# A graph network on one core: 38 of 98 edge groups of the second pass summed by dense one-hot products instead of gathered rows

## The reference, cut to what matters

```python
# 6250 nodes of 96 features, 100000 edges sorted by dst, 32 edge attributes
def L0(x, src, dst, edge_attr):
    edge_input = concat([x[src], edge_attr])
    messages = gelu(edge_input @ mW1 + mb1) @ mW2 + mb2
    gates = sigmoid(gelu(edge_input @ gW1 + gb1) @ gW2 + gb2)
    aggregated = segment_sum(messages * gates, dst)
    update = gelu(concat([x, aggregated]) @ uW1 + ub1) @ uW2 + ub2
    return layernorm(x + update) * ln_g + ln_b
def L1(x, src, dst, edge_weight):            # GCN layer, with self loops
    dinv = rsqrt(segment_sum(edge_weight, dst) + 1)
    return dinv * segment_sum(edge_weight * (x * dinv)[src], dst) @ W + self_loop_term + b
x = layernorm(x + L0(x, ...)); return layernorm(x + L1(x, ...))
```

## Time and profile before

| what | value |
|---|---|
| median of 3 runs | 2140.92 us (2139.51 to 2141.7) |
| the profiled execution's own time | 2138.67 us |
| span of the profile, first to last instruction | 2136.8 us |
| TensorE busy in the span | 1028.7 us (48%) |
| VectorE busy | 952.5 us (45%) |
| ScalarE busy | 388.2 us (18%) |
| GpSimd busy | 1599.9 us (75%) |
| mean granted TensorE clock | 0.678 of full speed |

### The profile page before, as it was taken

One profiled execution on the slowest core, in us unless ns is written; L12 is line 12 of the kernel. 1 busy time (PEld: TensorE's weight loads), 2 busy tenths in 40 slices (PEclk: granted clock), 3 DMA queues, 4 the chain that ended last, 5 costly groups with the idle time before them and its releaser, 6 DMA issues.

```text
span 2136.8 us, 22553 instructions
## 1 busy us (share of the span) xinstructions
PE 1028.7 (48%) x6513; PEld 960.2 (45%) x6514; DVE 952.5 (45%) x3023; ACT 388.2 (18%) x926; POOL 1599.9 (75%) x1577
## 2 busy tenths in 40 slices
PE   1378776767676676767732223322223332222223
PEld 1368776666666666656622222222222222222222
DVE  4248755565656565656641332323333232323323
ACT  1135433333333333333310000000000000000000
POOL 7777777777777777777627777777777777777775
PEclk9789988888888888888865555555555555555555
DMA  5222222222222222222201111211111111111111
GB/s 133 70 59 59 55 52 51 53 51 50 55 49 54 49 52 52 52 51 53 49 18 40 40 41 40 41 41 40 41 41 41 41 40 40 42 40 41 40 40 34
DMA packets 72963, 103.13 MB, mean 48 GB/s; under 512 B 42525, under 2 KB 44093, under 8 KB 72735
## 3 DMA queue, kind: packets, MB, share of 16 engines
q0 software_dynamic: 50048, 76.97, 17.1%
q10 hardware_dynamic: 18288, 17.26, 2.8%
q1 hardware_dynamic: 4496, 7.34, 1.2%
HBM read 96.65 MB, written 4.82 MB: 47 GB/s over the span
## 4 chain that ended last, share of the span: by engine, by line
POOL 74%; issue 22%; PE 1%; DVE 1%; DMA 0%; DVEq 0%; ACT 0%; POOLq 0%; ACTq 0%
POOL rows L299 74%; PE ps_win L350 0%; PE ps_hid L404 0%; DMA rows<-x1s_table,idx 0%; DMA x1s_table<-xs 0%; DMA rows<-in_x_nat,idx 0%; PE ps_hid L401 0%; PE ps_xt L379 0%; DVE vals L744 0%; DMA idx<-in_src_t 0%; PE ps_bt L440 0%; PE ps_bt L435 0%; PE ps_bn L447 0%; DVE step L730 0%; DVE step L728 0%
## 5 line engine op out<-in xcount | busy, mean ns | idle before, releaser
L299 POOL DMA_INDIRECT rows<-in_x_nat,idx x782 | 820.0, 1049 | 240.2 <-issue 237.9
L299 POOL DMA_INDIRECT rows<-x1s_table,idx x782 | 778.1, 995 | 280.5 <-issue 238.0
L350 PE MATMUL ps_win<-hot,rows 128*96 128x80 f32 x1568 | 279.2, 373 | 723.4 <-DMA rows<-x1s_table,idx 723.4
L350 PEld LDWEIGHTS ps_win<-hot,rows 128*96 128x96 f32 x1568 | 258.2, 277 | 745.9 <-DMA rows<-x1s_table,idx 745.9
L404 PE MATMUL ps_hid<-w,feat 128*128 128x192 f32 x1568 | 350.6, 350 | 0.0
L404 PEld LDWEIGHTS ps_hid<-w,feat 128*128 128x128 f32 x1568 | 297.3, 209 | 11.6 <-issue 0.8
L379 PE MATMUL ps_xt<-ident,rows 128*96 128x128 f32 x784 | 143.8, 344 | 318.4 <-DMA rows<-in_x_nat,idx 318.4
L379 PEld LDWEIGHTS ps_xt<-ident,rows 128*96 128x96 f32 x784 | 109.8, 158 | 335.5 <-DMA rows<-in_x_nat,idx 332.7
L531 ACT ACTIVATE hid<-ps_hid 128x384 f32<-128x384 f32 x392 | 192.2, 490 | 235.7 <-PE ps_hid L404 227.1
L863 DVE SCALAR_TENSOR_TENSOR h<-ps_bn,dinv,x1b 128x96 f32<-128x96 f32 x49 | 15.5, 318 | 485.9 <-PE ps_bn L505 485.8
L598 ACT ACTIVATE agg_t<-acc 96x128 f32<-96x128 f32 (+1 forms) x48 | 14.9, 311 | 1009.1 <-DVE y L878 957.8
(11 more groups left out here) (96 smaller groups left out, 799.1 us busy)
## 6 DMA issues: line engine op xcount, KB each, us to landing
rows<-in_x_nat,idx POOLq DMA_INDIRECT x782, 2.6
rows<-x1s_table,idx POOLq DMA_INDIRECT x782, 2.5
feat<-in_edge_t ACTq DMA_DIRECT2D x96, 128.0 KB, 2.3
x_t<-in_x_t SPq DMA_DIRECT2D x1, 2376.5 KB
out_nodes<-y ACTq DMA_DIRECT2D x48, 48.0 KB, 1.5
x1s_table<-xs ACTq DMA_DIRECT2D x47, 48.0 KB
dst_rows<-in_dst_rows SPq DMA_DIRECT2D x1, 392.0 KB
dst_i<-in_dst_t SPq DMA_DIRECT2D x1, 392.0 KB, 4.2
```

What stands on the lines that cost most here:

```text
L299: nc.gpsimd.indirect_dma_start(out=rows[g % SLOTS][:, k, :], out_offset=None, in_=table, in_offset=bass.IndirectOffsetOnAxis(ap=idx[:, TG ...
L350: mm = nc.tensor.matmul(ps_win[u][0:rws, 0:W], lhs[:, k, :], hot[u][:, k, :], start=(k == 0), stop=(k == TG - 1))
```

## The change

In pass 2 the 98 groups are dealt out in turns of five. Of the first 95 groups those with g % 5 equal to 0 or 3 are dense (`DENSE`, 38 groups), the other 60 are gathered as before (`GATHERED`).

A dense group fetches no rows. The table's rows stay in SBUF too (`x_nat` now holds them, block by block, written by `block1`). A source node is split into its block (`idx >> 7`) and its place in the block (`idx & 127`). For each of the 8 tiles VectorE makes the one-hot of the place (`raw_low`, half a group at a time, 128x512) and of the pair block and target (`hot_place`, 49 blocks x 12 targets in two halves of 300, half a group at a time, 128x2400). ScalarE multiplies the first by the edge weights, tile by tile (`weigh`, into `hot_low`). TensorE multiplies the two, 2 products of 300 columns for a tile, into two pairs of PSUM banks in turn, and ScalarE copies each result (128x600) to `dense_b`, rearranged by block. Then 49 products of 96 columns, one per block of `x_nat`, sum over all blocks into `ps_bt` (96 = 8 tiles x 12 targets). ScalarE copies that to `sum_rows`, and one product with `hot_node` puts it into the window (`place_sums`).

A tile's targets must lie within 12 nodes for this; the count of tiles that break it goes into the value that chooses between the written-out and the general branch. In the inputs no tile of a dense group spans more than 11 nodes, so the written-out branch is taken, as before.

A dense group's window is placed after that of the gathered group that follows it (`second_pass`). Blocks are finished in pairs (`PARTS`). `ps_win` is now a single buffer in both passes, so each window waits for the one before to be added. The second freed PSUM bank (`ps_fix`) holds constants that VectorE reads: the counting row 0 to 299 (before in SBUF as `iota_w`), the gate weights `gw2_ps`, the gate `gate_ps`, and in pass 2 the edge weights `weight_ps`. So in pass 1 and pass 2 VectorE's products over 640 and 768 elements now read one input from SBUF and one from PSUM. The general branch of pass 2 is unchanged in what it does. The prologue gains some twenty small VectorE instructions, two TensorE products, and a wider iota.

```diff
+WD = 12
+HH = -(-NB // 2)
+HW = HH * WD
+TW = TG * WD
+TURN = 5
+MIXED = NG // TURN * TURN
+DENSE = [g for g in range(MIXED) if g % TURN in (0, 3)]
+GATHERED = [g for g in range(NG) if g not in DENSE]
+def second_pass():
+    made, waiting = {}, None
+    for g in range(NG):
+        if g in DENSE:
+            waiting = g
+        else:
+            made[g] = [g] if waiting is None else [g, waiting]
+            waiting = None
+    order = [g for at in sorted(made) for g in made[at]]
+    place = {g: n for n, g in enumerate(order)}
+    added_at = {g: at + 1 for at in made for g in made[at]}
+    parts = []
+    for b in [0] + list(range(1, NB, 2)):
+        n = 1 if b == 0 else 2
+        needs = range(min(2 * (b + n - 1) + 3, NG))
+        parts.append((b, n, max(added_at[g] for g in needs), max(place[g] for g in needs) + 1))
+    return made, place, parts
+MADE, PLACE, PARTS = second_pass()
...
-        ps_win = [psum(f"ps_win{k}") for k in range(2)]
+        ps_win = psum("ps_win")
+        ps_fix = psum("ps_fix")
+        places_ps = ps_fix[:, 0:HW]
+        gw2_ps = ps_fix[:, HW:HW + ND]
+        gate_ps = [ps_fix[:, HW + ND + TG * u:HW + ND + TG * (u + 1)] for u in range(2)]
+        weight_ps = ps_fix[:, HW:HW + TG * WCH]
...
@@ gpsimd, second pass @@
+                for i, g in enumerate(GATHERED):
+                    if i >= SLOTS:
+                        pool.wait_ge(s_acc2, PLACE[GATHERED[i - SLOTS]] + 1)
+                    gathers(g, i % SLOTS, x1s_table, s_rows2)
...
@@ tensor @@
-                wait(pe, acc_sem, g - 1)
+                wait(pe, acc_sem, g)
...
+            def dense2(d):
+                for k in range(TG):
+                    if k % (TG // 2) == 0:
+                        pe.wait_ge(s_hot_d, 2 * d + 2 * k // TG + 1)
+                    pe.wait_ge(s_weighed, TG * d + k + 1)
+                    wait(pe, s_cellc, TG * d + k - 1)
+                    for m in range(2):
+                        mm = nc.tensor.matmul(ps_pair[k % 2][:, m, 0:HW], hot_low[:, k, :], hot_place[:, 2 * k + m, :],
+                                              start=True, stop=True)
+                    mm.then_inc(s_cells, 1)
...
+                wait(pe, s_rowsumc, d)
+                pe.wait_ge(s_cellc, TG * (d + 1))
+                for c in range(NB):
+                    mm = nc.tensor.matmul(ps_bt[0:TW, 0:ND], wide[:, TW * c:TW * (c + 1)],
+                                          x_nat[:, c, :], start=(c == 0), stop=(c == NB - 1))
+                mm.then_inc(s_rowsum, 1)
+            def place_sums(d, n):
+                pe.wait_ge(s_rowsumc, d + 1)
+                pe.wait_ge(s_hot_n, d + 1)
+                wait(pe, s_acc2, n)
+                nc.tensor.matmul(ps_win[0:ND, 0:W], sum_rows[d % 2][:, :], hot_node[d % 2][:, :],
+                                 start=True, stop=True).then_inc(s_win2[n % 2], 1)
+            def usual2():
+                for at in range(NG + 3):
+                    if at in DENSE:
+                        dense2(DENSE.index(at))
+                    for g in MADE.get(at, []):
+                        if g in DENSE:
+                            place_sums(DENSE.index(g), PLACE[g])
+                        else:
+                            gathered_sums(GATHERED.index(g), PLACE[g])
+                    for b, n, ready, _ in PARTS:
+                        if at == ready + 1:
+                            block2(b, n)
...
@@ scalar @@
+            def weigh(d, m):
+                act.wait_ge(s_raw, 2 * d + m + 1)
+                for q in range(TG // 2):
+                    k = TG // 2 * m + q
+                    wait(act, s_cells, TG * (d - 1) + k + 1)
+                    nc.scalar.activation(hot_low[:, k, :], raw_low[:, q, :], ACT.Copy,
+                                         scale=weight[:, TG * DENSE[d] + k:TG * DENSE[d] + k + 1]).then_inc(s_weighed, 1)
+            def dense2(d):
+                weigh(d, 0)
+                wait(act, s_rowsum, d)
+                for k in range(TG):
+                    if k == 2:
+                        weigh(d, 1)
+                    act.wait_ge(s_cells, TG * d + k + 1)
+                    nc.scalar.activation(dense_b[:, :, :, k, :], ps_pair[k % 2][:, :, 0:HW].rearrange("p h (c j) -> p h c j", j=WD), ACT.Copy).then_inc(s_cellc, 1)
+                act.wait_ge(s_rowsum, d + 1)
+                nc.scalar.activation(sum_rows[d % 2][:, :], ps_bt[0:TW, 0:ND], ACT.Copy).then_inc(s_rowsumc, 1)
...
@@ vector @@
-                    iota_w[:, :].rearrange("p (o w) -> p o w", o=1).to_broadcast([P, TG, W]), ALU.is_equal)
+                    places_ps[:, 0:W].rearrange("p (o w) -> p o w", o=1).to_broadcast([P, TG, W]), ALU.is_equal)
...
-                                        vals[u][:, :, ND:ND + 1].to_broadcast([P, TG, ND]), ALU.mult).then_inc(s_vals, 1)
+                                        column(gate_ps[u]).to_broadcast([P, TG, ND]), ALU.mult).then_inc(s_vals, 1)
...
-                                        gw2[:, :].rearrange("p (o c) -> p o c", o=1).to_broadcast([P, TG, ND]), ALU.mult)
+                                        gw2_ps.rearrange("p (o c) -> p o c", o=1).to_broadcast([P, TG, ND]), ALU.mult)
...
+            def dense2(d):
+                g = DENSE[d]
+                nc.vector.tensor_scalar(hot_node[d % 2][:, :], places_ps[0:TW, 0:W], node_of[:, g:g + 1], None,
+                                        ALU.is_equal).then_inc(s_hot_n, 1)
+                for m in range(2):
+                    ks = range(TG // 2 * m, TG // 2 * (m + 1))
+                    wait(dve, s_cells, TG * (d - 1) + ks[-1] + 1)
+                    wait(dve, s_weighed, TG * d + ks[0])
+                    nc.vector.tensor_tensor(raw_low[:, :, :], column(src_low[:, TG * d + ks[0]:TG * d + ks[-1] + 1]).to_broadcast([P, TG // 2, P]),
+                                            places_ps[:, 0:P].rearrange("p (o w) -> p o w", o=1).to_broadcast([P, TG // 2, P]),
+                                            ALU.is_equal).then_inc(s_raw, 1)
+                    cells = cell[:, TG * d + ks[0]:TG * d + ks[-1] + 1, :].rearrange("p k (h o) -> p (k h) o", o=1)
+                    nc.vector.tensor_tensor(hot_place[:, 2 * ks[0]:2 * ks[-1] + 2, :], cells.to_broadcast([P, TG, HW]),
+                                            places_ps.rearrange("p (o w) -> p o w", o=1).to_broadcast([P, TG, HW]),
+                                            ALU.is_equal).then_inc(s_hot_d, 1)
...
+            def usual2():
+                for at in range(NG + 3):
+                    if at in DENSE:
+                        dense2(DENSE.index(at))
+                    elif at < NG:
+                        gathered2(GATHERED.index(at), at)
+                    for g in MADE.get(at - 1, []):
+                        n = PLACE[g]
+                        take_window(acc1, ND, g, 0, True, s_win2[n % 2], n // 2 + 1, s_acc2, None, None, True)
+                    for b, n, ready, _ in PARTS:
+                        if at == ready + 2:
+                            block2(list(range(b, b + n)))
```

More of the change, by code:

```diff
@@ L211, in run_pass @@
             with eng.If(hard < 1):
-                for g in range(first, NG):
-                    step_fn(g // SLOTS, g % SLOTS, True, beside(g))
+                if usual is not None:
+                    usual()
+                else:
+                    for g in range(first, NG):
+                        step_fn(g // SLOTS, g % SLOTS, True, beside(g))
                 if end is not None:
@@ L295, in _, with gathers @@
         def _(pool):
-            def gathers(g, table, rows_sem):
+            def gathers(g, slot, table, rows_sem):
                 last = g == NG - 1
@@ L308, in _ @@
             pool.wait_ge(s_idx[0], 16)
-            gathers(0, t["x_nat"], s_rows)
+            gathers(0, 0, t["x_nat"], s_rows)
             n_const += const(nc.gpsimd.memset(ident[:, :], 0.0))
@@ L495, in step2 @@
                 window(g, u, easy, rows[v], ND, s_acc2, s_win2[u], s_far_hot2, s_far_win2)
-                if b is not None and not last:
-                    block2(b)
             def block2(b, n=1):
```

254 lines of the change are left out of this document (179 added, 75 removed).

## The result

The changed kernel takes **2163.27 us** (median of 4 runs, 2161.84 to 2164.8) against 2140.22 for the kernel before on the same chip: ratio 1.0109, 95% interval 1.0091 to 1.0126. It is 1.1% slower.

A forecast was written before the change was run, and what follows sets the result against it. Pass 2 becomes a ring of TensorE, VectorE and ScalarE, gathers no longer bounding it: 3.6 + 718 + 331 + 4 + 33 + 29 = 1119 us against 1032.5, +86; pass 1 -75; forecast 2152 us, range 2085 to 2235.

The forecast's parts named there:

- Pass 1: Gathers no longer stretched once VectorE's long products read one input from PSUM: gain 75 us, bounds 0 and 78.
- 6.8 us of it is one gather held by the clearing of the accumulator, which stays: Pass 1: part of the 85 us of gather stretching that the change would not remove.
- Tiles: TensorE's 8 one-hot tiles of a dense group in pass 2, with ScalarE's copies and weighing: 10.05 us a group.
- The rival in which ScalarE is the pace: Pass 2 tiles: ScalarE's copy takes 0.95 us, 1.7 us more a group, 65 us, time 2217; chance 0.12.
- Sum over blocks: TensorE's 98 records of 96 columns in a dense group, 0.09 us each: 8.8 us a group.
- Stops: TensorE's waits between dense groups in pass 2: 9 x 5.8 + 9 x 13.15 + 11 x 6.25 + 8 x 11.5 = 331 us.
- The first kind: Stops after a group with g % 5 = 3, no pair of blocks due: 5.8 us each, nine of them.
- block products and copies at the other places: Pass 2, between dense groups: a separate term of 4 us beside the 331 us of stops.
- The clock: TensorE's clock falling at stops in pass 2: 27 us for 17 stops and the start, 6 us more; 33 us, bounds 0 and 60.
- each stop of 6 us or more costs 1.5 us: Step of the clock term: 17 stops and the start, 27 us; of nine 4 us stops, half, 6 us.
- The rival with no loss and 2100 us: Ring runs lighter: clock stays at 2.4 GHz (-33), records stream at 0.085 us (-19); chance 0.21.
- Tail: End of pass 2: five windows, two pairs of blocks and the last output in sequence, 29 us from the last sum.

The follow-up runs named there:

- the ring order: Changed kernel, same 38 dense groups, reordered: VectorE makes the next dense group's one-hots before adding windows, ScalarE weighs around the sums' copy; 1874.65 us, ratio 0.8769.

## Why the prediction was right, and where its terms were off

- **Pass 1** (75 us predicted): the last gather starts at 984.0 us instead of 1061.5, 77.5. Right. The row that showed why it could be known was the reduction with one SBUF input that stretched nothing; the runs with the PSUM inputs alone and with them taken back show the cause. What the Trainium skill says (SBUF — State Buffer, Who interferes with whom) of instructions with at most one SBUF input agrees: the products with one PSUM input left gathers at 0.95 us. Its inference that tensor_tensor does not stall the making of descriptors does not carry over to these gathers, 947 against 1049 ns. An indirect gather also reads its indices (`idx`) from SBUF, and no run here tells whether that reading or the making of descriptors was held up.
- **"6.8 us of it is one gather held by the clearing of the accumulator, which stays"**: wrong. The clearing is there in the profile after, and no gather beside it is long:

```profile
29.13 5.42 DVE L844 MEMSET acc<- 98x6432 f32 x1 [1.29 <-issue]
```

  The gather at 29.98 us took 0.95 us, and none was long there in the profiles of the changed kernel and the nine others. So 6.8 of the 77.8 us went with no cause shown, and what is left for the PSUM inputs is 71, not 75; undoing them cost 65. The errors nearly cancel, and that is luck.
- **Tiles** (10.05 us a group): 10.1 where the clock was up. ScalarE's copy of 600 elements, extrapolated to 665 ns, took 667; `hot_place` 2644 ns (2650). Two parts of the 10.05 were off and cancel, which is luck too: a tile takes 1.05 us and not 1.01, and the weighing between two tiles costs 0.63 us (10.07 against 9.44 in the ring order, which has none) and not 0.95. The rival in which ScalarE is the pace did not come.
- **Sum over blocks** (8.8 us each, 334): 8.4, 318. I priced a record by a window's, 0.09 us with a load of 98 columns; it takes 8.54 / 98 = 0.087, and the next group of records starts before the last one ends. The Trainium skill's rule on loads and products with the same rows (TensorE: Matmul & The Clock Gate, Packing small matmuls) would have made this 15.7 us a group; the trace disagrees, 8.54. The same section also lets a load into the background weight buffer run ahead, which would allow what the trace shows.
- **Stops** (331 us): 337.5. By kind, predicted and measured: 9 x 5.8 = 52 and 58.1; 9 x 13.15 = 118 and 118.6; 11 x 6.25 = 69 and 68.7; 8 x 11.5 = 92 and 92.1. The first kind came out high in four of the nine, 6.9 us and not 5.8: there a pair's products (L589, 1.09 us at a granted clock of 0.50) stand between the placing and the tile, and ScalarE copies the pair's sums (L725) before it weighs. The prediction had put such products and copies into a term of their own, the 4 us of "block products and copies at the other places"; with it 335 stand against 337.5. The stops were worked out from durations of before and the order of the programs, and they carried the prediction.
- **The clock** (33 us) was the term that was mis-sized, and it more than makes up the 11 us: cells took 441.5 us, and 38 x 10.1 is 384, so the clock cost 57, 24 more than the term. I charged 17 stops and half of nine; in fact 33 of 38 cells phases began slow, also behind 15 of the 20 stops of 5.6 to 7 us. Over all cells the granted clock was 0.50 for 136 us. A slow phase cost 1.7 us (57 / 33) and not 1.5. The step that was short is "each stop of 6 us or more costs 1.5 us", which counted a stop by its idle time and left out the eleven 6 us stops after g % 5 = 0, broken by a window and a placing. The rival with no loss and 2100 us failed on the same point, though not everywhere: behind the first five stops without a block after g % 5 = 0 the clock was still up, behind the six later ones it was not.
- **Tail**: 31 us from the last sum (29 predicted).

Cells, sums and stops are the whole stretch from the first tile to the last sum (441.5 + 318 + 337.5 = 1097). The misses in sum: clock +24, tiles +2, stops with the blocks at other places +2, sums -16, pass 1 -2.5, tail +2 give +11.5, against 2160.0 - 2148 = 12 in the span. The mechanism was the one forecast; that the time came within 0.5% owes something to luck, since the sums over blocks took back two thirds of what the clock added. And one more miss of the size of the clock's, downwards, and the kernel would have been no slower: with the terms this far from certain, chances of 0.58 and 0.36 were what the rows could bear.

## What to carry to other kernels

Before work is taken off the engine that bounds, lay the engines that take it over in one line of handovers and add up the stops; here 304 gathers fewer bought nothing until the order let the next group's one-hots be made during this group's products, and then 289 us. When two changes travel together, run each alone: the PSUM half is worth 120 us and hid that the dense groups cost 143. Choose the share of moved work last: the order decides where the two engines balance, and of the 38, 32 and 28 dense groups that were tried in the ring order 28 were best.

## What the runs showed of the hardware

- A gather of GpSimd (128 rows) is 0.94 to 0.95 us beside VectorE products with one PSUM input and up to 1.74 beside those with two SBUF inputs; with the operands of pass 1 put back into SBUF, its 782 gathers took 65 us more.
- TensorE's clock fell behind stops that weren't idle throughout. These are the first records after stops of the same length, 6.0 us, of which the last 1.72 us were idle, early and late in pass 2 of the changed kernel:

```profile
1109.27 1.28 PE L599 MATMUL ps_xt<-edges 128*128 128x300 f32 x4 [1.72 <-DVE edges L1064]
...
1811.04 2.37 PE L599 MATMUL ps_xt<-edges 128*128 128x300 f32 x4 [1.72 <-DVE edges L1064]
```

  The first ran at a granted clock of 1.00 (2.4 GHz) and the second at 0.50 (1.2 GHz). In the changed kernel half clock was paid behind 33 stops or starts, for 4.1 us each in the mean (136 / 33). In the ring order, with stops of 2.1 to 4.6 us, only the first of 38 cells phases was slow. What sets apart two stops that look alike stays open.
- The 7.77 us gather beside the clearing of the accumulator was seen once, in the kernel before, and not again in ten later profiles. Its cause is open.
